# The second attention of a two-layer transformer on one core: turns four heads behind, GpSimd behind the norm, VectorE's copies moved, the turns of q and k wider apart

## The reference

```python
x = _layernorm(x + _L0_attn_ref(x, ...))   # 16 heads, polynomial attention, blocks of 256 tokens
x = _layernorm(x + _L0_ffn_ref(x, ...))    # silu(gate) * up, down
x = _layernorm(x + _L1_attn_ref(x, ...))   # the part that changes here
x = _layernorm(x + _L1_ffn_ref(x, ...))    # 8 experts, top 2, and a shared expert

# _L1_attn_ref: 32 heads of 8 numbers, softmax with a bias of relative positions
q, k, v = heads(x @ wq.T), heads(x @ wk.T), heads(x @ wv.T)
scores = einsum('bhqd,bhkd->bhqk', q, k) / sqrt(8) + rel_bias
attn = softmax(scores)
out = (attn @ v).reshape(B, S, 256) @ wo.T
```

## Time and profile before

| | |
|---|---|
| median of 3 runs | 1031.82 us (1025.96 to 1033.84) |
| the profiled execution's own time | 1028.5 us, span 1026.6 us |
| PE busy | 888.6 us (87%) |
| VectorE busy | 716.0 us (70%) |
| ScalarE busy | 682.8 us (67%) |
| GpSimd busy | 285.5 us (28%) |
| mean granted TensorE clock | 0.965 |
| second attention (first to last `least`) | about 379 to 795 us of the span |
| costliest group on ScalarE | L1428, the exponentials, 232.2 us |
| costliest group on VectorE | L1951, `least`, 191.2 us |
| PE's turns of heads, L933 | 161.1 us, with 37.0 us of idle time ahead of them |

### The profile page before, as it was taken

One profiled execution on the slowest core, in us unless ns is written; L12 is line 12 of the kernel. 1 busy time (PEld: TensorE's weight loads), 2 busy tenths in 40 slices (PEclk: granted clock), 3 DMA queues, 4 the chain that ended last, 5 costly groups with the idle time before them and its releaser, 6 DMA issues.

```text
span 1026.6 us, 21001 instructions
## 1 busy us (share of the span) xinstructions
PE 888.6 (87%) x7200; PEld 715.4 (70%) x7200; DVE 716.0 (70%) x2092; ACT 682.8 (67%) x1475; POOL 285.5 (28%) x373
## 2 busy tenths in 40 slices
PE   4666899999899988898988898988888899799994
PEld 3455787788788985565666666666655788698884
DVE  6778877877865557788887877788877553265437
ACT  2675766857764349888888787888888323266644
POOL 1347632323432202002020202010101217434436
PEclk8888999999999999999999999999999999899997
DMA  6203022010000102011110101110011302244444
GB/s 186 62 2 104 1 74 83 12 32 22 12 31 22 42 11 64 2 26 39 26 40 26 40 25 40 26 31 24 22 32 50 98 15 101 83 109 115 114 131 163
DMA packets 58569, 54.87 MB, mean 53 GB/s; under 512 B 17921, under 2 KB 54017, under 8 KB 58466
## 3 DMA queue, kind: packets, MB, share of 16 engines
q1 hardware_dynamic: 55058, 44.18, 14.9%
q0 software_dynamic: 3408, 9.34, 2.7%
HBM read 32.85 MB, written 20.65 MB: 52 GB/s over the span
## 4 chain that ended last, share of the span: by engine, by line
PE 45%; DVE 21%; ACT 15%; issue 10%; POOL 5%; DMA 3%; SPq 1%; DVEq 0%; ACTq 0%; POOLq 0%
PE ps L434 8%; PE ps L435 7%; PE ps L436 7%; ACT G L1428 6%; PE ps L933 5%; DVE G L1951 4%; PE ps L648 4%; POOL xs L2404 3%; PE ps L950 3%; PE ps L921 3%; ACT G L1438 2%; DVE RT L1754 1%; PE ps L719 1%; PE ps L663 1%; PE ps L1115 1%
## 5 line engine op out<-in xcount | busy, mean ns | idle before, releaser
L1428 ACT ACTIVATE G<-G,small 128x256 f32<-128x256 f32 x512 | 232.2, 509 | 54.3 <-DVE small L1951 52.9
L1951 DVE CUSTOM_DVE_ANT_0 G<-ps,nb 128x256 f32<-128x256 f32 x512 | 191.2, 420 | 74.7 <-PE ps L921 74.4
L933 PE MATMUL ps<-ident,G 128*128 128x128 f32 x1024 | 161.1, 287 | 37.0 <-ACT G L1428 34.5
L933 PEld LDWEIGHTS ps<-ident,G 128*128 128x128 f32 x1024 | 111.2, 143 | 74.0 <-ACT G L1428 57.9
L434 PE MATMUL ps<-WU 128*128 128x256 f32 x384 | 117.1, 305 | 14.5 <-DVE WU L1768 5.0
L1438 ACT COPY G<-ps 128x512 f32<-128x512 f32 x192 | 111.4, 580 | 13.2 <-PE ps L933 13.2
L2311 POOL TENSOR_SCALAR_AFFINE_SELECT G<-G 128x256 f32<-128x256 f32 x128 | 76.4, 621 | 152.9 <-ACT G L1283 152.6
L435 PE MATMUL ps<-WU 128*128 128x256 f32 x384 | 108.3, 282 | 0.0
L436 PE MATMUL ps<-WU 128*128 128x256 f32 x384 | 108.2, 282 | 0.0
L2273 POOL TENSOR_SCALAR small<-small 128x2 f32<-128x2 f32 x16 | 6.6, 412 | 342.3 <-DVE small L1605 342.3
L434 PEld LDWEIGHTS ps<-WU 128*128 128x128 f32 x384 | 72.7, 189 | 22.5 <-DVE WU L1781 8.4
(11 more groups left out here) (245 smaller groups left out, 2230.7 us busy)
## 6 DMA issues: line engine op xcount, KB each, us to landing
xs<-G SPq DMA_DIRECT2D x8, 645.0 KB, 6.8
G<-xs SPq DMA_DIRECT2D x39, 128.0 KB
G<-in_x SPq DMA_DIRECT2D x16, 256.0 KB, 2.9
G<-x SPq DMA_DIRECT2D x16, 256.0 KB, 3.1
wu_rows<-yy SPq DMA_DIRECT2D x8, 512.0 KB, 7.4
x<-G SPq DMA_DIRECT2D x15, 256.0 KB, 3.0
wu_rows<-in_wu SPq DMA_DIRECT2D x8, 384.0 KB, 6.1
wraw<-in_wu SPq DMA_DIRECT2D x8, 256.0 KB, 2.9
```

Source lines behind the costliest of these rows:

```text
L933: m = pe.transpose(ps[:, 2 + h % 2, S * kt + P * t:S * kt + P * (t + 1)], prob(h)[:, t, P * kt:P * (kt + 1)], ident[:])
L1428: m = act.activation(prob(h)[:, t, :], prob(h)[:, t, :], ACT.Exp, scale=-1.0, bias=mneg[:, k:k + 1])
L1951: m = dve.tensor_tensor_reduce(prob(h)[:, t, :], ps[:, SCORE_BANKS[h % 3], S * t:S * (t + 1)], nbv[:, t, :], 1.0, -FMIN, ALU.add, ALU.min, ...
```

## The change

- **Turns four heads behind.** `TURN_LAG = 4`: at head `h` PE turns head `h - 4` and no longer `h - 2`; `mix` moves by two heads too; ScalarE and VectorE take `h - 4`. A head now stays longer in its buffer, so `prob` gets seven buffers instead of four. The three new ones lie in the place of expert 7's weights, whose gate and up part is therefore loaded and split after the attention, behind the shared expert's last tiles.
- **GpSimd's wait.** Behind `layernorm_rstd` GpSimd waits for `xo_ready`, that is, for the norm itself, before the next split.
- **VectorE's order.** `take` stands behind `least` of the same head instead of ahead of it. It stays ahead of everything else that VectorE does at head `h`.
- **The tables.** The third and fourth turn of q and k stand at heads 1 and 5 instead of 1 and 3, `x_turn` at 7 instead of 5, `qk` at 10 and 15 instead of 8 and 14, and most of the rest one or two heads later.

The diff, cut to its core:

```diff
-PE2 = dict(heads=(25, 29, 1, 3), x_turn=5, qk=(8, 14), c_turn=(6, 8, 10, 12), ct_turn=17, v=19,
-           project=21)
-ACT2 = dict(heads=(26, 30, 1, 4), place_v=5, x_hi=5, context_hi=18, hi_parts=(9, 15), stage_v=20)
-DVE2 = dict(heads=(26, 30, 1, 4), outputs=(12, 20, 28, 4), x_lo=7, context=(7, 9, 11, 13),
-            context_lo=19, add=23, norm=25, lo_parts=(11, 17))
+PE2 = dict(heads=(26, 30, 1, 5), x_turn=7, qk=(10, 15), c_turn=(8, 10, 12, 14), ct_turn=17, v=20,
+           project=22)
+ACT2 = dict(heads=(27, 31, 2, 6), place_v=7, x_hi=8, context_hi=18, hi_parts=(11, 16), stage_v=21)
+DVE2 = dict(heads=(27, 31, 2, 6), outputs=(14, 22, 30, 6), x_lo=9, context=(9, 11, 13, 15),
+            context_lo=19, add=24, norm=26, lo_parts=(12, 18))
+TURN_LAG = 4
+PROBS = 7
...
-        def prob(h):
-
-            return WORK[:, 512 * (h % 4):512 * (h % 4 + 1)].rearrange("p (t k) -> p t k", t=2)
+        def prob(n):
+
+            slot = n % PROBS
+            late = EX_AT + 2 * EX * (NEXP - 1) + 512 * (slot - 4)
+            buf = WORK[:, 512 * slot:512 * (slot + 1)] if slot < 4 else wu_rows[:, late:late + 512]
+            return buf.rearrange("p (t k) -> p t k", t=2)
...
PE, in one(i, first, left):
-                        if h >= 2 or not first:
-                            turn(i, h - 2, first)
-                        if h % 4 == 3 and (h > 3 or not first):
-                            mix(i if h > 3 else i - 1, (h - 7) // 4 % 8, first)
+                        if h >= TURN_LAG or not first:
+                            turn(i, h - TURN_LAG, first)
+                        if h % 4 == 1 and (h >= 9 or not first):
+                            mix(i if h >= 9 else i - 1, (h - 9) // 4 % 8, first)
ACT, in one:
-                        if on_act(h - 2) and (h >= 2 or not first):
-                            take(i, h - 2, first)
+                        if on_act(h - TURN_LAG) and (h >= TURN_LAG or not first):
+                            take(i, h - TURN_LAG, first)
                         exponential(i, h, first)
DVE, in least and in one:
-                    if h >= 4 or not first:
-
-                        dve.wait_ge(probT_turned, H2 * i + h - 3)
+                    if h >= PROBS or not first:
+
+                        dve.wait_ge(probT_turned, H2 * i + h - PROBS + 1)
...
-                        if not on_act(h - 3) and (h >= 3 or not first):
-                            take(i, h - 3, first)
                         least(i, h, first)
+                        if not on_act(h - TURN_LAG) and (h >= TURN_LAG or not first):
+                            take(i, h - TURN_LAG, first)
POOL:
             for i in range(iterations[2]):
-                expert_part(i, 0)
+                if i < iterations[2] - 1:
+                    expert_part(i, 0)
                 shared_part(i)
                 if i < iterations[2] - 1:
                     expert_part(i, 1)
                     layernorm_rstd(2, i, 2)
+                    pool.wait_ge(xo_ready, NORMS[2] + i + 1)
...
             layernorm_rstd(2, iterations[2] - 1, 2)
+            pool.wait_ge(xo_ready, NORMS[2] + iterations[2])
 
             pool.wait_ge(y_ready[2], iterations[2])
-            split(LOADS3 - 1, PARTS3 - 1, shared(SH_KEPT, 0, 0, UNIT), shared(SH_KEPT, 1, 0, UNIT), wraw[:])
...
+            split(LOADS3 - 2, PARTS3 - 2, shared(SH_KEPT, 0, 0, UNIT), shared(SH_KEPT, 1, 0, UNIT), wraw[:])
...
+            expert_part(NEXP - 1, 0)
+            expert_part(NEXP - 1, 1)
```

63 lines of the change are left out of this document (38 added, 25 removed).

## The result

The changed kernel takes 1020.98 us (median of 9 runs, 1019.48 to 1022.72) against 1031.82 (median of 9, 1025.85 to 1035.99). The ratio is 0.9901 with a 95% interval of 0.9873 to 0.9929, some 10 us faster (the medians differ by 10.8). The forecast was 1003, so the sign was right and less than half of the gain came.

What follows compares the result with a forecast made beforehand. No engine is full; PE, VectorE and ScalarE wait for each other in a ring. Seven blocks 22.4, block 0 1.5, clock 4.5, less 1 and 1, take 26.4 us off 1028.5: 1002, called 1003 for the median; full range 984 to 1022.

Steps and rivals of the forecast that it cites:

- The norm: Second attention: GpSimd's wait ends the norm's collision with a split, saving 1.23 us in each of seven blocks.
- Four heads behind: PE's turns in the attention: longer lag covers nearly all waits for exponentials; 3.2 us saved a block, norm's 1.23 included.
- the blocks at both ends: Ends of the attention: block 0, without a norm, saves 1.5 us; two more turns at the end cost about 1.
- The tables: Other moved entries in the attention: they even out load between scores; taken at 0, between -0.5 and +0.5 us a block.
- The sum: Whole kernel: blocks 22.4, block 0 1.5, clock 4.5, less 1 and 1, together 26.4 us saved.
- The tokens' turn: PE's turn of the next tokens: its wait for ScalarE's copy of turned q stays, 1.2 to 1.6 us.
- The clock: Attention: three of seven falls to 1.2 GHz, those behind the norm, go, saving 4.5 us; four stay.
- The experts' stage: Behind the attention: splits run later but under 8 us of cover; collisions with VectorE cost 0 to 3, taken as 1.
- the "about 37": Expected sign in the experts' stage: GpSimd done with the last split about 37 us behind the attention's end.
- Only the norm: Rival, chance 0.15: turns wait for banks, so the longer lag brings nothing; 1017 to 1021 us, say 1020.
- It does nothing: Rival, chance 0.10: norm's time passes to another wait, new distances cost the lag's gain; time stays within 1%.
- what would make the prediction wrong: Attention: turns waiting 3 us or more a block, tokens' turn over 2.5, or ScalarE and VectorE waits at new distances.

Runs made afterwards that it cites:

- norm_only: Kernel before with only GpSimd's wait for the norm added; ratio to before 0.9901.
- no_norm_wait: Changed kernel without GpSimd's waits for the norm; ratio to before 1.0033.
- lag_two: Changed kernel with turns two heads behind instead of four, all else kept; ratio to before 1.0154.
- wide_lag2: wide_lo with turns two heads behind instead of four; ratio to before 0.9861.
- wide: heads_3 with the tokens' high part on ScalarE at head 7 instead of 8; ratio to before 0.967 (one run).
- wide_lo: wide with VectorE's first low part of q and k at head 13 instead of 12; ratio to before 0.9642.
- heads_3: Changed kernel with q and k's fourth turn at head 3 (was 5), its copies at 4, the third's copies one head earlier; ratio to before 0.974 (one run).
- old_tables: Changed kernel with table entries set back to the old heads wherever the lag of four allows; ratio to before 1.0214.
- order_only: norm_only with VectorE's `least` ahead of `take`, which now takes head h - 2 instead of h - 3; ratio to before 0.988 (one run).
- after_again: Changed kernel without any edit, repeated on a fourth chip; ratio to before 0.9892.
- wide_pv: wide_lo with the placing of v on ScalarE at head 6 instead of 7; ratio to before 0.960 (one run), repeated 0.9578, 1011.54 us.

## Why the prediction was right or wrong, point by point

**The norm: right.** Forecast 1.23 us a block off the path. The pair takes 0.73 us and GpSimd's split begins behind it, first VectorE's row, then GpSimd's:

```profile
474.49 0.73 DVE L1637 TENSOR_SCALAR G<-G,small 128x256 f32<-128x256 f32 x2
```

```profile
475.28 0.77 POOL L2273 CAST WU<-wraw 128x704 fp32r<-128x704 f32 x1 [1.55 <-DVE G L1637]
```

`norm_only` gives 1.4 a block, `no_norm_wait` gives back 1.5 to 1.8. No wait of another engine for a split appears among those of the attention.

**Four heads behind: right in kind, too large for the block and too small for the stage.** Forecast 3.2 with the norm's 1.23, so 2.0 for the lag. Measured 1.46 (`lag_two`) and 1.7 (`wide_lag2`). With the blocks at both ends, the lag was to give 13.8 + 1.5 - 1 = 14.3 us; with the falls that go with it, it gives 24 in both pairs of kernels, most of the surplus in block 0, in the last block and in the clock. The rows that it rested on, 28.7 us of waits for exponentials, went as said, and what took part of their place was the banks, also as said: 9.1 us for ScalarE's copies and 2.9 for VectorE's, 1.7 a block, where 0.9 had been left for all remaining waits but the tokens' turn.

**The tables: this is the step that failed.** It said that "the other moves change the load between two scores by less than they even out: taken at 0, between -0.5 and +0.5 us a block", and that the chains "keep at least one head between an engine and the next". Measured +2.6 at a lag of two, with the place of `mix`. The chains do keep one head between them, and at a lag of four one head is too little. ScalarE's high part at head h stands behind its exponential of h, while VectorE, with `least` of h + 1 done, is already at the low part. The profile of before could have said so: there the tokens' parts stood at heads 5 and 7 and those of q and k at 9 and 11, two heads apart, and the trace of before has one short wait of PE for the context in blocks 1 to 7, and none for a low part:

```profile
PE ps L663 <- DVE G L1632: 0.2, 1, 0.2
```

The change takes both distances from two to one (8 and 9, 11 and 12). `wide` and `wide_lo` set just these two back to two and win 0.7 and 1.2 us a block, at a lag of four and with `heads_3` in place. At a lag of two these two distances are not shown to make up the 2.6 us: VectorE's waits for the high parts are only 0.9 us (tokens) and 3.2 (q and k) in `lag_two`, against 8.6 and 6.8 in the changed kernel. The sum had a second fault: it added the lag and the tables as independent terms, and `old_tables` shows that they are not. I compared the load between scores and did not write the distances of the tables, old and new, side by side.

**The sum.** Seven blocks were to give 3.2 each. Along the path of the runs (before, `norm_only`, `order_only`, `lag_two`, changed) a full-clock block gives 1.4 (norm) + 0 (order) - 2.6 (tables, `mix`, buffers) + 1.5 (lag) = 0.25, which is 51.97 less 51.72. These steps add up by construction, and on another path, by way of `old_tables`, lag and tables would have other prices. The whole attention, falls and ends included, shows the same on a larger scale:

| us off the attention | forecast | along the runs |
|---|---|---|
| norm, with its three falls | 13.1 | 12.4 |
| order | in the lag's term | 0.8 |
| tables, `mix`, buffers | 0 | -27.7 |
| lag, with both ends | 14.3 | 24.1 |
| together | 27.4 | 9.6 |

So the term put at 0 cost more than the whole gain that was forecast, and the lag gave 10 us more than forecast, which covered a third of that. That 7 x 2.6 = 18.2 is nearly the 18.0 by which the forecast of 28.8 exceeds the measured 10.8 is chance. These are single profiles; the ratios of `norm_only` (0.9901), `lag_two` (1.0154) and the changed kernel (0.9901) bear both large steps out, 2.5% up and down again. Block 0 gave 1.4 (forecast 1.5) in this profile; in that of `after_again`, with two falls in it, it took 48.8 us and gave nothing.

**The tokens' turn: right.** Forecast 1.2 to 1.6:

```profile
598.01 0.66 PE L629 MATMUL ps<-ident,G 128*128 128x128 f32 x4 [1.43 <-ACT RT L1220]
```

The reason given, that it needs `least`, exponential and copy whatever the lag, was right for this table. But that the change "does not shorten" it was taken for more than it is: `heads_3` takes it away by giving the copy two more heads.

**The clock: right in number, in part by luck.** Seven falls to four, as forecast. Of the three that were put down to the norm, the two at 579.9 and 634.5 have no counterpart in `norm_only`. The third, at 788.1, has: `norm_only` falls at 774.5, at the same place of the last block, behind the same two short waits of PE (0.44 and 0.63 us), though its norm takes 0.73 us there. It is gone in the changed kernel and in `wide_lo`, and `lag_two` and `wide_lag2` have falls in the last block, so it is the lag that takes it away. Of the four behind the copy of the turned q (the one at 757.4 stood at the scores, since the last block has no tokens' turn) three are left, at or just behind the tokens' turn (493.8, 599.6 and 650.8 us, the turns at 493.3, 598.0 and 650.6). The fourth lies in block 0, where before had none. `after_again` also has four, but two of them in block 0. In the full blocks a fall makes the block 1.2 to 1.4 us longer in the kernel before and 0.9 to 1.2 in the changed one.

**The experts' stage: right.** GpSimd's splits and the scatter in the timeline of the changed kernel:

```profile
811.24 0.82 POOL L2273 CAST AW<-wraw 128x768 fp32r<-128x768 f32 x1 [3.96 <-DVE G L1637]
...
829.67 1.29 POOL L2278 TENSOR_TENSOR WU<-wraw,WU 128x512 fp32r<-128x512 f32 x1
...
838.97 1.24 POOL L2430 DMA_INDIRECT xs<-G,small  x1 [8.01 <-DVE small L2119]
```

The first split waits 3.96 us for the norm. The last one is over at 831.0, 42.6 us behind the last `least`; the working gave 837 in the time of before, 42.3 behind it (the "about 37" in the prediction's last paragraph was miscounted). The scatter still waits 8.0 us for VectorE. It begins 50.6 us behind the last `least`, against 50.2 before (844.87 - 794.7): 0.4 us, where 1 had been taken for collisions. The trace shows one collision on this chain. VectorE's comparison with two SBUF inputs (L2075) falls into the last split, which had begun 0.4 us before it and ends at 831.0; the same instruction of before (L2054) had no split beside it. First the changed kernel, then before:

```profile
830.04 1.07 DVE L2075 TENSOR_TENSOR G<-G 128x128 f32<-128x128 f32 x1
```

```profile
836.70 0.29 DVE L2054 TENSOR_TENSOR G<-G 128x128 f32<-128x128 f32 x1
```

It takes 0.78 us longer. The Trainium skill's rule, page "SBUF — State Buffer", section "SBUF: two separate sides", that VectorE with two SBUF inputs waits for a GpSimd instruction that began first, agrees with this; that it would make the term 3 did not come true, because VectorE was held once.

**The rivals.** *Only the norm* named 1020, the time that was measured, for a reason that is wrong. It held that turns wait for banks and the lag brings nothing, while the lag brings 1.5 us a block and the tables take more than that away. That the two cancel was no case of mine, and that 1020 was met is luck. *It does nothing* came nearest in its half sentence on "the new distances". And the last condition under what would make the prediction wrong, waits at "the tokens' high part at 8, low part at 9; q's and k's parts at 11 and 12", is what happened, both pairs as named: the place was seen, but no price was put on it.

**What stays open.** Which entries make up the 2.6 us. The four mended ones give 4.3 together, more than the change had lost, since the tokens' wait was there before. How much of the loss each new entry brought at a lag of two was not parted, nor the tables from `mix` and the buffers. Nor is it shown why old tables and a lag of four go so badly together. The last block's 3.0 us come with the lag (it takes 51.3 us in `lag_two` and 44.9 in the changed kernel, 49.0 in `wide_lag2` and 42.9 in `wide_lo`); why the lag is worth more there than in the other blocks is not shown beyond the two falls that go.

## What to carry to other kernels

Where the order of several engines is written out by hand, list for each chain the distance between maker and user, before and after an edit. Here one head between two engines cost a wait in every block, two did not, and four table entries moved by one or two heads gave three times the gain of the whole change. A longer lag was worth the same in two sets of places and, by all signs, a loss in a third, so the price of one part holds for the others as they stand, and the gain of one can hide the loss of another. Undo or add each part by itself, from both ends, before a change is kept or dropped as a whole. And when the total agrees with a forecast, look whether its terms do.

## What of the hardware was not expected

- **A collision of VectorE and GpSimd leaves no wait in the profile.** The norm of two instructions took 2.22 us and takes 0.73 when GpSimd stays away; the profile shows a longer instruction and a stretch in which nothing is waited for the earlier trace rows. The Trainium skill, page "SBUF — State Buffer", section "SBUF: two separate sides", tells of a lock that is held for a whole instruction, so that the other engine waits for its end. `norm_only` and `no_norm_wait` agree with it, with 0.49 and 1.89 us for the longest norm, and in the earlier trace rows the norm's first instruction ends just behind GpSimd's subtraction. The page also has the one that starts first take the lock; here VectorE's recorded start is the earlier one, by 0.07 us (574.44 against 574.51), and it is VectorE that is held. The recorded starts don't show which of the two has the lock.
- **The clock fell behind waits of PE far shorter than the fall.** In the kernel before and in the changed one single waits of 1.4 us stand ahead of falls. In blocks 2 to 4 of `wide_lag2` no wait of PE is over 0.72 us, and each has a fall, one of them at 508.4 us, behind two waits close together, as PE's timeline shows:

```profile
507.08 0.66 PE L949 MATMUL ps<-ident,wu_rows 128*128 128x128 f32 x4 [0.71 <-ACT wu_rows L1446]
507.67 0.50 PE L937 MATMUL ps<-RT 32*128 32x256 f32 x4
508.36 0.86 PE L949 MATMUL ps<-ident,wu_rows 128*128 128x128 f32 x3 [0.19 <-ACT wu_rows L1446]
```

  `heads_3` and `wide`, with single waits of 1.3 us, have none in blocks 1 to 7, and neither have `wide_lo` and `wide_pv`, whose longest is 0.9. So the longest wait alone does not decide it. What does was not tried. A fall makes the block 0.9 to 1.2 us longer in the changed kernel and 1.6 in `wide_lag2`.
- **Blocks at full clock repeat within 0.05 us**, over executions and over chips: 51.72 and 51.74 in two profiles of the changed kernel, 47.45 and 47.44 of `wide_pv`. Such a block is a far finer measure than the kernel's time, in which the chips differ by 2%. Nearly all of that lies behind the attention: 231 and 254 us in the two profiles of the changed kernel, 232 and 256 in those of `wide_pv`. But it leaves out the falls and the ends: the lag, worth 1.5 us a full-clock block, that is 9 in blocks 1 to 6, was worth 24 in the attention.
